# A mixture's last shared unit behind its experts, and the next stage's head inside the tail of the stage before

## The reference

```python
x = x + 0.5 * _L0_ffn_ref(_layernorm(x), ...)     # stage 0: mixture, 1 shared + 7 routed experts
x = x + _L0_attn_ref(_layernorm(x), ...)          # stage 1: landmark attention
x = x + 0.5 * _L0_ffn_ref(_layernorm(x), ...)     # stage 2: the same mixture again
x = x + 0.5 * _L1_ffn_ref(_layernorm(x), ...)     # stage 3: mixture of 16 experts, tokens chosen by Sinkhorn
x = x + _L1_attn_ref(_layernorm(x), ...)          # stage 4: quaternion attention
x = x + 0.5 * _L1_ffn_ref(_layernorm(x), ...)     # stage 5
```

## Time and profile before

| | us |
|---|---|
| runs (3) | 2939.17, 2945.19, 2945.19; median 2945.19 |
| profiled execution, own time | 2939.72 |
| its span, first to last instruction | 2938.0 |
| mean granted TensorE clock | 0.982 |
| stage 0, mixture, ends (last matmul) | about 679 |
| stage 1, attention, ends | about 1041 |
| stage 2, mixture, ends | about 1710 |
| PE busy, share of the span | 95% |

### The profile page before, as it was taken

The page is one execution under the profiler, slowest core; times in us unless marked ns, Lnnn a source line. Parts: engine busy times, 40 slices in busy tenths (PEclk is TensorE's granted clock), DMA queues, the critical chain, the costliest instruction groups (busy, mean ns, idle before and its releaser), DMA issues.

```text
span 2938.0 us, 55357 instructions
## 1 busy us (share of the span) xinstructions
PE 2794.0 (95%) x22775; PEld 2189.7 (75%) x22775; DVE 1843.3 (63%) x3753; ACT 1634.8 (56%) x2460; POOL 541.2 (18%) x478
## 2 busy tenths in 40 slices
PE   9999999997999999999999978997999999998998
PEld 7889999996767778889999956995433434333898
DVE  7775555558887687755555477875535463436776
ACT  4434455543443344344545424775798878892776
POOL 0002224121000000022232254552000000001343
PEclk9999999999999999999999999999999999998999
DMA  4223333232000022133333344773442252513675
GB/s 153 74 65 112 93 86 87 79 84 74 2 3 23 3 69 80 65 112 91 85 84 86 82 141 143 201 197 101 97 130 53 64 117 63 123 37 116 187 205 141
DMA packets 237853, 279.72 MB, mean 95 GB/s; under 512 B 23811, under 2 KB 219040, under 8 KB 237600
## 3 DMA queue, kind: packets, MB, share of 16 engines
q1 hardware_dynamic: 205296, 228.75, 26.3%
q0 software_dynamic: 30720, 45.85, 8.0%
q10 hardware_dynamic: 1584, 1.57, 0.2%
HBM read 204.58 MB, written 72.88 MB: 94 GB/s over the span
## 4 chain that ended last, share of the span: by engine, by line
PE 75%; DVE 14%; ACT 5%; issue 4%; DMA 2%; POOL 1%; DVEq 0%; POOLq 0%; ACTq 0%
PE PS L162 17%; PE PS L163 16%; PE PS L164 16%; PE PS L2939 12%; PE PS L1028 6%; PE PS L170 2%; DVE SM L194 1%; ACT FW L547 1%; ACT Z L582 1%; PE PS L511 1%; DVE SM L1403 1%; PE PS L500 1%; DVE FW L624 1%; PE PS L3032 1%; ACT P L3089 1%
## 5 line engine op out<-in xcount | busy, mean ns | idle before, releaser
L3089 ACT ACTIVATE P<-PS 128x1024 f32<-128x1024 f32 x512 | 485.0, 1045 | 97.1 <-PE PS L2939 95.4
L162 PE MATMUL PS<-FH,FW 128*128 128x366 f32 (+1 forms) x1408 | 506.0, 359 | 7.4 <-ACT SIL L533 6.1
L163 PE MATMUL PS<-FH,FW 128*128 128x366 f32 (+1 forms) x1408 | 497.3, 353 | 0.0
L164 PE MATMUL PS<-FH,FW 128*128 128x366 f32 (+1 forms) x1408 | 495.4, 352 | 0.0
L541 ACT ACTIVATE FHH<-PROD 128x366 fp32r<-128x366 f32 (+1 forms) x352 | 194.4, 552 | 415.4 <-DVE PROD L612 415.0
L162 PE MATMUL PS<-FW,FHH 128*122 128x256 f32 (+1 forms) x1184 | 338.8, 286 | 1.5 <-DVE FHH L619 1.5
L163 PE MATMUL PS<-FW,FHH 128*122 128x256 f32 (+1 forms) x1184 | 333.2, 281 | 0.0
L164 PE MATMUL PS<-FW,FHH 128*122 128x256 f32 (+1 forms) x1184 | 333.1, 281 | 0.0
L612 DVE TENSOR_TENSOR PROD<-SIL,PS 128x366 f32<-128x366 f32 (+1 forms) x352 | 206.9, 588 | 171.3 <-PE PS L164 169.5
L619 DVE TENSOR_TENSOR FHH<-PROD,FHH 128x366 fp32r<-128x366 f32 (+1 forms) x352 | 208.8, 593 | 142.2 <-ACT FHH L541 142.2
L162 PEld LDWEIGHTS PS<-FH,FW 128*128 128x128 f32 x1408 | 264.7, 188 | 30.7 <-ACT SIL L533 10.6
(11 more groups left out here) (461 smaller groups left out, 5591.8 us busy)
## 6 DMA issues: line engine op xcount, KB each, us to landing
WS<-L_ffn_w_dram SPq DMA_DIRECT2D x256, 256.0 KB, 3.7
WST<-L_ffn_W_dram SPq DMA_DIRECT2D x168, 256.0 KB, 3.5
S<-parts_scratch SPq DMA_DIRECT2D x60, 384.0 KB, 8.3
parts_scratch<-PT SPq DMA_DIRECT2D x28, 512.0 KB, 4.1
WST<-L_ffn_W1s_dram SPq DMA_DIRECT2D x40, 256.0 KB, 2.7
WST<-L_ffn_W3s_dram SPq DMA_DIRECT2D x40, 256.0 KB, 3.5
WST<-L_ffn_W2s_dram SPq DMA_DIRECT2D x40, 256.0 KB, 4.0
xa_scratch<-X SPq DMA_DIRECT2D x17, 512.0 KB, 5.0
```

Source lines behind the costliest of these rows:

```text
L162: e.matmul(o, lh, rh, start=start, stop=False, skip_group_check=True)
L163: e.matmul(o, ll, rh, start=False, stop=False, skip_group_check=True)
L164: return e.matmul(o, lh, rl, start=False, stop=stop, skip_group_check=True)
L3089: e.activation(self.PR[K % 3][:, 2 * jj:2 * jj + 2, :].rearrange("p a b -> p (a b)"), c.pair(2 * ((2 * K + jj) % 3)), ACT.Exp, scale=0.25) ...
```

## The change

- In the mixture the order becomes u0, u1, u2, seven experts, u3 half 0, u3 half 1. The copies back (`xget`) are issued in step 2 of the last unit but one, in order 0 to 7. The routing moves a slot or more forward, since the experts begin eight half steps earlier. Both halves of u3 are added after the copies have come back, and x of these tokens goes to DRAM without a shared part.
- The mixture has 11 rooms: the 15th, 12th, 11th, 9th, 7th, 6th, 5th, 4th, 3rd and 2nd `up` from the end and the last `down` but one. The last two units have eight `up` each, so the 15th from the end is step 1 of the last unit but one. The class is used for both calls.
- The landmark attention has 11 pieces, all that comes before its first `qk`: the weights' load and their rounding, `wl`, `cv`, statistics, root, normalisation and transposes of batch 0. Its memory is laid out anew, and new waits guard what it overlays.
- The attention has ten rooms in its tail, and the second mixture ten pieces for them: two weight loads, statistics of eight tiles, root, normalisation, the first `wt` and the first four transposes (`tp`), which now go through a buffer of their own and banks 0 to 3. The second call's load of gain, bias and router weights and 5 of its fill matmuls go.
- `Ffn1` is not changed but for `xput`, which sends eight tiles of the last batch instead of four; its two pieces meet the first two of the mixture's 11 rooms.

The diff, cut to what the steps below speak of:

```diff
@@ -295,8 +300,8 @@
             "p (x c t) -> p x c t", x=2, c=2) for k in range(2)]
         self.XR, self.YO = ([zf[:, o + 1536 * k:o + 1536 * k + 1536].rearrange("p (t d) -> p t d", d=D)
                              for k in range(2)] for o in (0, 3072))
-        self.units = ([(None, u, (0, 1)) for u in range(3)] + [(None, 3, (0,))] + [(e_, None, (0, 1)) for e_ in range(E0)] +
-                      [(None, 3, (1,))])
+        self.units = ([(None, u, (0, 1)) for u in range(3)] + [(e_, None, (0, 1)) for e_ in range(E0)] +
+                      [(None, 3, (0,)), (None, 3, (1,))])
         self.steps = 8 * len(self.units)
...
@@ -323,7 +330,9 @@
             if it[0] == "xget":
                 counts[self.back(it[2])] = 16
             p.count(it, counts)
-        self.rooms = self.ups[-1], ("xs", call, len(self.units) - 1)
+        self.rooms = tuple(self.ups[-k] for k in (15, 12, 11, 9, 7, 6, 5, 4, 3, 2)) + (("down", call, self.steps - 2),)
+        c.left = {"rows": ("ax", ("xt", call, E0 - 1, 3)), "stored": ("zo", ("zput", call, 7)), "added": ("sca", ("sca", call, E0 - 1)),
+                  "tokens": ("up", ("up", call, self.last_step(E0 - 1), 1)), "banks": ("xs", ("xs", call, len(self.units) - 2))}
         c.back = {b: (self.back(2 * b), ("xget", call, min(2 * b + 1, 6))) for b in range(4)}
 
     @staticmethod
@@ -333,12 +342,13 @@
 
     def order(self):
         n = self.call
-        self.ahead = [[("ld", n, 0), ("ld", n, 1), ("stats", n, 0, 4)], [("stats", n, 4, 8)]]
-        seq = [("consts", n), *self.ahead[0], *self.ahead[1], ("root", n, 0, 8)]
-        seq += [("norm", n, i, i + 4) for i in (0, 4)] + [("wrr", n), ("wt", n, 0), ("fill", n, 8 if self.first else 2)]
-        seq += [("tp", n, h, c) for h in range(2) for c in range(2)] + [("fill", n, 5 if self.first else 3)]
+        tps = [("tp", n, h, c) for h in range(2) for c in range(2)]
+        self.ahead = [[("ld", n, 0), ("ld", n, 1), ("stats", n, 0, 4)], [("stats", n, 4, 8)], [("root", n, 0, 8)],
+                      [("norm", n, 0, 4)], [("norm", n, 4, 8)], [("wt", n, 0)], tps[:1], tps[1:2], tps[2:3], tps[3:]]
+        seq = [("consts", n)] + [it for piece in self.ahead[:5] for it in piece]
+        seq += [("wrr", n), ("wt", n, 0)] + [("fill", n, 8)] * self.first + tps + [("fill", n, 5)] * self.first
         slots = [[] for _ in range(72)]
-        slots[0].append(("lg", n, 0))
+        slots[1].append(("lg", n, 0))
         slots[2].append(("lg", n, 1))
         slots[13].append(("best", n, 0))
...
-        slots[65].append(("tab", n))
-        slots[66] += [("xr", n, 0), ("xr", n, 1)]
+        slots[62].append(("tab", n))
+        slots[63] += [("xr", n, 0), ("xr", n, 1)]
+        for k in range(4):
+            slots[68 + k].append(("xt", n, 0, k))
+        slots[46].append(("xput", n, 6))
...
@@ -379,8 +392,6 @@
                 sl = [[], [], []]
                 if ui < 3:
                     sl = slots[3 * s:3 * s + 3]
-                elif ui == 3 and 2 <= j < 6:
-                    sl[2] = [("xt", n, 0, j - 2)]
                 elif e_ is not None and e_ + 1 < E0 and 3 <= j < 7:
                     sl[1] = [("xt", n, e_ + 1, j - 3)]
                 for h in hs:
@@ -394,10 +405,10 @@
                     k = s // 2
                     seq += [("ld", n, k + 2)] if k + 2 < self.steps // 2 else []
                     seq += [("wt", n, k + 1)] if k + 1 < self.steps // 2 else []
-                if j == 2 and 1 <= ui <= 4:
-                    seq += [("xput", n, q) for q in ((2 * ui - 2, 2 * ui - 1) if ui < 4 else (6,))]
-                if j == 2 and ui == last:
-                    seq += [("xget", n, q) for q in (7, *range(7))]
+                if j == 2 and 1 <= ui <= 3:
+                    seq += [("xput", n, q) for q in (2 * ui - 2, 2 * ui - 1)]
+                if j == 2 and ui == last - 1:
+                    seq += [("xget", n, q) for q in range(8)]
                 if e_ is not None and j == 1 and e_ + 2 < E0:
                     seq.append(("xr", n, e_ + 2))
                 seq += sl[2]
...
@@ -481,7 +492,9 @@
             ins.then_inc(*p.one("sl"))
         elif k in ("tp", "lg", "tot", "pos", "xt"):
             early = k == "tp" and it[2] < 2
-            pb = c.bank(4 + 2 * it[2] + it[3] if early else 3)
+            pb = c.bank(2 * it[2] + it[3] if early else 3)
+            if early and self.spent:
+                w.wait_ge(*p.at(*self.spent["banks"]))
             if it in self.bank_before and not early:
                 before = self.bank_before[it]
...
@@ -544,13 +555,17 @@
             w.wait_ge(*p.at(f"wl{q % 2}", ("ld", n, q)))
             if q >= 2:
                 w.wait_ge(*p.at("dn", ("down", n, 2 * q - 3)))
+            elif self.spent:
+                w.wait_ge(*p.at(*self.spent["values"]))
             e.activation(self.FW[:, q % 2, 0, :], self.WST[:, q % 2, :], ACT.Copy).then_inc(*p.one("wh"))
         elif k in ("tp", "xt"):
             early = k == "tp" and it[2] < 2
             h, cc = it[2:] if k == "tp" else divmod(it[3], 2)
             nh = 512 if k == "tp" else 366
             if early:
-                src, full = c.bank(4 + 2 * h + cc), (self.PROD if h else self.SIL)[:, cc, :]
+                src, full = c.bank(2 * h + cc), self.TMP[:, 2 * h + cc, :]
+                if self.spent:
+                    w.wait_ge(*p.at(*self.spent["rows"]))
             else:
                 src, full = c.bank(3, nh), self.aux_of[it][:, 0:nh]
                 if it in self.aux_before:
...
     PARTS = slice(0, 512), slice(512, 768)
     QUAD = "kl", "na", "nt", "la", "lt"
     ORDER = """
-        stats00 stats01 root00 stats02 nrm00 stats03 root01 nrm01 ht001 ht000 wl0 ht011 ht010 qk000 wl1 cv0 stats10
-        stats20 stats13 lm000 stats11 qk010 na010 qk001 lm010 na000 qk011 lm001 la010 lm011 vv03 na001 vv00 stats12
-        na011 vv02 nm0 kl0 root10 nt010 nrm11 nrm10 vv01 stats30 nt000 stats21 ht111 ht101 ht110 ht100 la001
-        nc00 ksa0 nt011 stats23 ksb0 qk100 stats31 la000 qk101 stats22 nt001 kt0 lx00 lm101 den0 nd00 la011
+        wl0 wl1 cv0 stats00 stats01 stats02 stats03 root00 nrm00 nrm01 ht001 ht000 ht011 ht010 qk000 lm000
+        qk010 qk001 lm010 na010 stats10 lm001 qk011 na000 stats13 vv03 lm011 la010 vv00 na001 stats11 vv02 stats12
+        na011 vv01 nm0 kl0 root10 nt010 nrm11 nrm10 stats20 nt000 ht111 ht101 ht110 ht100 la001
...
-        self.ahead = [self.items[2:4], self.items[4:5]]
-        self.rooms = ("lc", call, 3, 0, 0), ("le", call, 3, 3)
+        named = lambda names: [self.item(x) for x in names.split()]
+        self.ahead = [[("wget", call)], [("wa", call)], named("wl0 wl1"), named("cv0"), named("stats00 stats01"),
+                      named("stats02 stats03"), named("root00"), named("nrm00"), named("nrm01 ht001"), named("ht000 ht011"),
+                      named("ht010")]
+        self.rooms = tuple(map(self.item, "iw32 iw33 iw34 le23 lc300 ld300 ld301 lc310 ld310 le30".split()))
...
+        c.top_free = last("pp", ("nc", 0), ("nc", 1))
+        c.spent = {"values": c.top_free, "banks": ("fa", ("lt", call, 3, 1, 1)),
+                   "rows": last("pp", *(("vv", k) for k in range(4)), *(("qk", *x) for x in ALL4))}
 
     def order(self):
...
@@ -1204,13 +1239,19 @@
             e.preload_act_table_set("natural_log_exp_and_others")
             return
         if k == "wa":
-            w.wait_ge(*p.at("aw", ("consts", n)))
+            w.wait_ge(*p.at("aw", ("wget", n)))
+            if self.left:
+                w.wait_ge(*p.at(*self.left["rows"]))
             for cs in self.PARTS:
                 e.activation(self.WAS[:, 0, :, cs], self.WA[:, :, cs], ACT.Copy).then_inc(*p.one("wah"))
+            return
...
@@ -1298,6 +1339,8 @@
         bc = lambda v, m: v.unsqueeze(2).broadcast_to([128, v.shape[1], m])
         if k == "cv":
             w.wait_ge(*p.at("ident", ("start",)))
+            if self.left:
+                w.wait_ge(*p.at(*self.left["added"]))
             w.wait_ge(*p.mine())
             e.tensor_reduce(self.IND, c.IDENT[:, :].rearrange("p (t j) -> p j t", j=32), AX,
                             ALU.add).then_inc(*p.one("dv"))
...
@@ -1500,8 +1545,12 @@
 
     def sp(self, e, w, it):
         p, A = self.c.p, self.c.A
-        if it[0] == "consts":
+        if it[0] == "wget":
+            if self.left:
+                w.wait_ge(*p.at(*self.left["rows"]))
+                w.wait_ge(*p.at(*self.left["stored"]))
             e.dma_start(self.WA[:, :, :], cpf(A["L0_attn_W_attn"])).then_inc(*p.dma("aw"))
+        elif it[0] == "consts":
             e.dma_start(self.WP[:, :, :], cpf(A["L0_attn_W_proj"])).then_inc(*p.dma("ap"))
 
```

More of the change, by code:

```diff
@@ L263, in __init__ @@
         self.top_free, c.top_free = c.top_free, ()
+        self.spent, c.spent = c.spent, {}
+        if first:
+            c.weighed = "consts", call
         z_at = c.at
@@ L314, in __init__ @@
             counts = dict(self.COUNTS.get(it[0], {}))
```

(22 more changed lines are left out.)

94 lines of the change are left out of this document (52 added, 42 removed), and 3 rows, old and new, of the table COUNTS.

## The result

| | before | changed |
|---|---|---|
| runs, median | 2945.19 us (4 runs, 2939.17 to 2947.93) | 2983.89 us (4 runs, 2981.66 to 2986.62) |
| profiled execution: own time, span | 2939.72, 2938.0 | 2981.66, 2979.9 |

The ratio is 1.0131, with a 95% interval of 1.0118 to 1.0143: **38.7 us slower, where 10.8 (2956) had been forecast**. The sum itself was made against the profiled execution: +16 there, and 42 measured. The sign was right, the size was not, and the time lies outside the range.

The account below looks back on a forecast made before the run. PE was busy 95% of the span, with DVE bounding the first border. From the profiled execution, 2939.7 - 4 + 0 + 0 + 20 = 2955.7, say 2956 us; own range 2948 to 2965, 8-in-10 range 2944 to 2968.

Parts of the forecast that it names:

- The stop in the second mixture: Last unit but one: early statistics wait for copies of x, PE stands 18.6 us, then half clock; +20 in sum.
- The routing at 0, upper end +1.5 for each call: Routing a few slots earlier in both mixture calls: first expert's rows still land in time; 0, at most +1.5 us each.
- The border to the attention at -4: First mixture to attention, head moved into the mixture's tail: `nm` comes 4 us ahead; ends 0 and -11.9.
- The term for stops in the tail: First mixture's last two units: PE waits for DVE's pieces of the attention's head, 4.7 us in sum.
- The border to the mixture at 0: Attention to second mixture: the head in the tail costs there what it saves behind the meet; 0, ends -9.2 and +4.
- The rest at 0: Second call's small tensor load, 5 fill matmuls and the larger `xput`: 0, since none ends a wait.
- The rivals: Three alternatives: no stop in the second mixture (2935, chance 0.06), heads fully hidden (2939, 0.06), costlier tails (2967, 0.12).
- The tails give way: Rival: first border 0, second +4, routing +3, second mixture's stop +20, giving 2967; chance 0.12.

Follow-up runs that it names:

- Even rooms: Most of the first mixture's pieces moved out of half steps behind a `wt`, against changed kernel with later second gather, late second-call rooms, small matmuls apart: 2943.75 us.
- the list of before: Attention's order behind the head put back to that of the kernel before the change, against the kernel with Even rooms: 2941.34 us, ratio 0.9994.

## Why the prediction was wrong, step by step

- **The stop in the second mixture: right.** Forecast +20, from a stop of 18.6 us; the trace has 18.98, the kernel without it is 17.5 us faster (15 by the ratios). The copy landed later (6.9 us behind the first issue instead of 5.8), and POOL issued it sooner than counted (13.7 us behind the last expert's first addition instead of 14.0).
- **The routing at 0, upper end +1.5 for each call: wrong, and the largest miss.** It cost 7 us in each call of the profiled execution, 14 of the 26 us by which its sum was missed: a stop of 4.8 to 5.0 us and half clock behind it. The step asked only whether the first expert's rows had landed and what its transposes cost. Behind that gather POOL issues the second expert's, without a break, and it now ran beside the first `xt`. In the trace of before the second expert's rows have landed by 1283.1, 10.8 us before the first `xt`; that distance was gone with the change, and the step named neither it nor its price. No row of before could have given the price, since no mark of PE is late in that trace; by what path the gather holds the marks back stays open.
- **The border to the attention at -4: mis-sized.** Taking off what was late already (2.0 at the start and 7.2 in the routing), the first `qk` comes when it did before, instead of 4 us sooner, and `nm` 0.6 us later. The term for stops in the tail was 4.7 us; PE lost 7.4 there, because six of the eleven rooms are in the half step behind a `wt`, which the step had seen as a danger for single pieces and then summed too low. Even rooms got 3 of the 4 us back in the trace. From `qk` to `nm` the step had 3.5 us more than for a start without DVE's backlog; by the list of before (26.3 us against 30.8) 4.5 of that stretch are the new list's price.
- **The border to the mixture at 0: right for the border, and yet +6.1 in that stretch, more than its upper end of +4.** What the head saves behind the meet (9.3 us) it costs in the tail, as forecast, with the same waits (ACT's `wt` ahead of the exponentials, DVE 4.16 us idle for it). The 6 us are from the attention's new list, whose cost the prediction had looked at only up to `nm` of the first batch.
- **The rest at 0.** It held, but for the small matmuls side by side, which are part of the routing's forward shift: 2 to 4 us in each call, all but 0.4 of it made up for within the same stretch. At the very start 2.0 us more belong to the single execution: of the 14 profiled ones, four have the first `up` at 21.2 to 21.5 and ten at 19.5 to 19.7, among kernels with the same start.
- **The rivals.** "The tails give way" (2967, with +3 for routing) had the direction, and 17 us too little. No rival took a gather as a cause, so the range could not reach 2984.

## What to carry to other kernels

When a step of a queue is moved forward, all that is queued behind it on the same engine moves too: look up what that next transfer used to run beside, and what it will run beside now. Work put into another stage's tail should stand where its engines are idle, not at even distances: the same head was worth nothing in one set of rooms and 4 us in another. An early reader of data that comes back late stops everything behind it in its engine's queue; pair pieces and rooms by what they wait for.

## What the runs showed of the hardware

- In nine of the fourteen traces PE's semaphore marks came late while gathers on POOL's queue were under way, and ACT's wait on a finished `down` of PE ended late with them. At the first expert's start it was 0.01, 1.32 and 5.72 us with none, three and six parts of the second gather under way, and about the same in the second call. The gathers' own transfers went on, and so did PE's matmuls until one needed ACT. Beside the gathers for the second and third expert, marks were up to 4.4 us late in six of these traces, with idle stretches of 0.2 to 0.6 us. In the other five traces, of the kernel before and of four kernels on one chip, no mark was late beside any gather. What the second condition is, and by what path the marks are held back, isn't settled.
- The TensorE clock fell to half with PE idle for no more than 0.31 us, behind 32 matmuls of 16 columns in a row (0.83 as the mean of 20 to 40 us), and stayed at full when 12 large ones stood between the two halves. The Trainium skill, page "TensorE: Matmul & The Clock Gate", section "What's actually happening", says that the slow clock is the default and that activity lifts it. The trace agrees in so far as idle gaps can't explain this fall; it also shows that PE can be busy in the profile (19.69 of 20 us) and lose the full clock.
